# Expert up products of 128 + 64 contracted rows, and the first bias added by ScalarE behind the turning

## What is computed

```
xm = _ln(x, ln2_g, ln2_b).reshape(B * S, D)           # 32 * 82 rows of 192
probs = softmax(xm @ router_w.T + router_b)
topw, topi = top_k(probs, 2); topw = topw / sum(topw)
for e in range(8):
    h = gelu(xm @ w1[e] + b1[e], approximate=False)   # 192 -> 768
    y = h @ w2[e] + b2[e]                             # 768 -> 192
    out = out + combine[:, e:e + 1] * y
x = x + out
```

## Time and profile before

| | |
|---|---|
| runs | 1379.35 us median of 3 (1374.2 to 1379.79) |
| the profiled execution | 1381.3 us, its span 1379.5 us, mean granted clock of TensorE 0.941 |
| TensorE (PE) busy, share of the span | 1219.3 us, 88% |
| VectorE (DVE) | 1016.1 us, 74% |
| GpSimd (POOL) | 742.8 us, 54% |
| ScalarE (ACT) | 686.8 us, 50% |
| of the costliest groups, in the expert stage: L2258 up | 143.6 us |
| L2277 down | 109.3 us |
| L2267 flip | 40.0 us |
| L2309 affine | 38.3 us |
| L2315 Gelu | 38.9 us |
| L2347 copy to hT | 46.0 us |

### The profile page before, as it was taken

How to read it: one execution, slowest core, us unless ns; L and a number is a source line. 1 busy time by engine, 2 the same in 40 slices (tenths; PEclk the granted TensorE clock), 3 DMA queues, 4 the chain that set the end, 5 groups by cost and what they waited for, 6 DMA issues and landing times.

```text
span 1379.5 us, 19671 instructions
## 1 busy us (share of the span) xinstructions
PE 1219.3 (88%) x5828; PEld 787.5 (57%) x5829; DVE 1016.1 (74%) x2150; ACT 686.8 (50%) x1467; POOL 742.8 (54%) x469
## 2 busy tenths in 40 slices
PE   7976876659898989899987789999999899999996
PEld 4432343225454545545443568888888677777774
DVE  5998797989899999999999646778788553333332
ACT  1355433576777777686855246545452332222221
POOL 3147642886869696969788300145455474222222
PEclk9997878798999999999999999999998699999998
DMA  6200012340413223140410001122122132222221
GB/s 183 59 1 0 31 34 97 96 147 15 133 50 98 70 77 111 36 146 0 146 33 1 1 31 42 43 67 59 56 69 71 33 68 46 37 38 36 36 36 21
DMA packets 72801, 81.19 MB, mean 59 GB/s; under 512 B 13282, under 2 KB 64705, under 8 KB 72721
## 3 DMA queue, kind: packets, MB, share of 16 engines
q1 hardware_dynamic: 53386, 69.29, 15.9%
q0 software_dynamic: 17152, 9.24, 4.9%
q10 hardware_dynamic: 2184, 1.72, 0.5%
HBM read 48.87 MB, written 30.01 MB: 57 GB/s over the span
## 4 chain that ended last, share of the span: by engine, by line
PE 60%; DVE 20%; ACT 10%; issue 6%; POOL 2%; DMA 1%; DVEq 0%; SPq 0%; ACTq 0%; POOLq 0%
PE ps L2258 10%; PE ps L1040 7%; PE ps L2277 7%; DVE hs L1324 6%; PE ps L1642 3%; PE ps L1700 3%; PE ps L951 3%; PE ps L1715 3%; PE ps L275 2%; PE ps L2267 2%; ACT ps L1193 2%; PE ps L268 2%; PE ps L1017 2%; DVE ps L205 2%; PE ps L976 2%
## 5 line engine op out<-in xcount | busy, mean ns | idle before, releaser
L1442 POOL TENSOR_TENSOR Bx<-dtz,Bb 128x984 f32<-128x984 f32 x128 | 288.2, 2270 | 45.8 <-DVE hs L1324 31.8
L1324 DVE TENSOR_TENSOR_SCAN hs<-ps,Bx 128x492 f32<-128x492 f32 x256 | 287.6, 1164 | 21.9 <-POOL Bx L1442 12.6
L1193 ACT ACTIVATE ps<-dt,A 128x324 f32<-128x324 f32 (+1 forms) x512 | 211.5, 456 | 79.2 <-DVE hs L1324 77.0
L1040 PE MATMUL ps<-hs,b_id 128*128 128x492 f32 x512 | 238.6, 589 | 12.0 <-DVE y L1291 9.3
L2377 POOL DMA_INDIRECT out<-yt,dest x48 | 74.7, 1556 | 168.8 <-DVE yt L2363 156.4
L1334 DVE TENSOR_TENSOR hs<-hs,ps 128x984 f32<-128x984 f32 x128 | 150.2, 1174 | 2.5 <-issue 0.6
L2258 PE MATMUL ps<-W,xT 97*128 (+1 forms) x384 | 143.6, 518 | 2.9 <-issue 1.6
L1040 PEld LDWEIGHTS ps<-hs,b_id 128*128 128x128 f32 x512 | 93.0, 195 | 79.6 <-issue 74.2
L2347 DVE COPY hT__6147<-ps 128x768 f32<-128x768 f32 x48 | 46.0, 958 | 111.3 <-PE ps L2267 108.8
L2277 PE MATMUL ps<-W,hT__6147 128*128 x576 | 109.3, 327 | 0.8 <-DVE yb L2357 0.8
L2315 ACT ACTIVATE hb<-ps 128x768 f32<-128x768 f32 x48 | 38.9, 810 | 142.5 <-PE ps L2258 142.5
(11 more groups left out here) (277 smaller groups left out, 2404.1 us busy)
## 6 DMA issues: line engine op xcount, KB each, us to landing
Bb<-b_rows SPq DMA_DIRECT2D x32, 656.0 KB, 6.7
buckets<-b_zero SPq DMA_DIRECT2D x8, 2288.0 KB, 15.2
xg<-buckets SPq DMA_DIRECT2D x48, 104.0 KB, 1.9
xc<-in_xcol SPq DMA_DIRECT2D x4, 1176.0 KB, 9.3
W<-in_w1d SPq DMA_DIRECT2D x8, 582.0 KB
W<-in_w2d SPq DMA_DIRECT2D x8, 576.0 KB
out<-H SPq DMA_DIRECT2D x8, 246.0 KB
H<-P SPq DMA_DIRECT2D x8, 147.0 KB
```

The source lines that it names most:

```text
L1040: mm = pe.matmul(ps[:, BANK_Y + h, 0:HALF], ident[:], f2(hs[:, s % LONG])[:, h * HALF:(h + 1) * HALF], start=s == 0, stop=s == STATE - 1)
L1193: a = act.activation(ps[:, BANK_A + h, c:c + w].rearrange("p (g t) -> p g t", t=S)[:, :, 1:S], dt[:, (par + t // STATE) % 2, m, g0 * S:g1 ...
L1324: v.tensor_tensor_scan(f2(hs[:, t % LONG])[:, c], ps[:, BANK_A + h, 0:HALF], f2(Bx[:, t % RING])[:, c], 0.0, ALU.mult, ALU.add).then_inc(s ...
L1442: g.tensor_tensor(Bx[:, t % RING], dtz[:, p], Bb[:, p, t % STATE, :].rearrange("p (a n) -> p a n", a=1).broadcast_to([128, NI, N]), ALU.mu ...
```

## The change

- The turned tile lies as 128 x 128 (columns 0 to 127 of the row) and, from columns 64 to 191, once more 128 x 128, of which the upper 64 partitions are columns 128 to 191. ScalarE writes `xT` in three activations: all 128 rows; the 64 upper rows to partitions 64 to 127; the same 64 rows to partitions 0 to 63.
- W1 is laid out as 128 rows of all 768 columns, and behind them 384 more columns that hold the last 64 rows: of columns 0 to 383 in partitions 0 to 63, of columns 384 to 767 in partitions 64 to 127. For the second half VectorE copies the 64 x 384 of the tile's expert to `wh` (`high_rows`).
- The up is two products of 128 rows, one for each half h, and then two of 64 rows, at partitions 0 to 63 for h = 0 and 64 to 127 for h = 1. TensorE waits for `wh` as well.
- The bias leaves W1. VectorE copies the result of the up to `hb` unchanged (ScalarE does so for tiles 0 and 1, `lift`). After the flips ScalarE writes `hT` with six Gelus of 128 x 128, each with its column of `b1` as the bias; b1 now lies along the partitions. VectorE's copy to `hT` is gone.
- ScalarE's step j is now hidden(j), affine(j+2); before, it was hidden(j+1), affine(j+2). ScalarE reads the tile's expert from `te`. In the interleaved part hidden(0) moves behind affine(2).
- VectorE's step j: the copy to `hb` of tile j+1, high_rows(j+2), keep_tail(j+2), then the output of down(j-1) as before.
- One more DMA loads `b1` (128 x 48 numbers), behind that of b2. The memory has places for `wh` and `e_b1`.

```diff
                 for k in range(2):
-                    mm = pe.transpose(ps[0:HD, turned(j), k * 128:(k + 1) * 128], xg[:, p, k * HD:(k + 1) * HD], ident[:])
+                    mm = pe.transpose(ps[:, turned(j), k * 128:(k + 1) * 128], xg[:, p, k * 64:k * 64 + 128], ident[:])
                 mm.then_inc(s_tx, 1)
 
             def up(j, p, e):
 
                 pe.wait_ge(s_xT, j + 1)
-                if isinstance(j, int) and j == 0:
-                    pe.wait_ge(s_cst, 1)
+                pe.wait_ge(s_wh, j + 1)
                 at_least(pe, s_ge, j)
                 for h in range(2):
-                    for k in range(2):
-                        c_ = slice(0, HD + k)
-                        mm = pe.matmul(ps[:, UP + h, 0:384], xT[c_, p, k, :],
-                                       W1[c_, k, bass.ds(e, 1), h * 384:(h + 1) * 384].rearrange("p a n -> p (a n)"),
-                                       start=k == 0, stop=k == 1)
+                    pe.matmul(ps[:, UP + h, 0:384], xT[:, p, 0, :],
+                              W1[:, bass.ds(e, 1), h * 384:(h + 1) * 384].rearrange("p a n -> p (a n)"), start=True, stop=False)
+                for h in range(2):
+                    half = slice(64 * h, 64 * h + 64)
+                    w = wh[half, p, :] if h else W1[half, bass.ds(e, 1), DFF:W1_ROW].rearrange("p a n -> p (a n)")
+                    mm = pe.matmul(ps[:, UP + h, 0:384], xT[half, p, 1, :], w, start=False, stop=True)
                 mm.then_inc(s_h, 1)
...
             def affine(j, p):
                 act.wait_ge(s_tx, j + 1)
-                for k in range(2):
-                    a = act.activation(xT[0:HD, p, k, :], ps[0:HD, turned(j), k * 128:(k + 1) * 128], ACT.Identity,
-                                       bias=vec[0:HD, V_LN2_B + k:V_LN2_B + k + 1], scale=vec[0:HD, V_LN2_G + k:V_LN2_G + k + 1])
+                high = slice(64, 128)
+                act.activation(xT[:, p, 0, :], ps[:, turned(j), 0:128], ACT.Identity, bias=vec[:, V_E_B:V_E_B + 1], scale=vec[:, V_E_G:V_E_G + 1])
+                for rows in (high, slice(0, 64)):
+                    a = act.activation(xT[rows, p, 1, :], ps[high, turned(j), 128:256], ACT.Identity,
+                                       bias=vec[high, V_E_B + 1:V_E_B + 2], scale=vec[high, V_E_G + 1:V_E_G + 2])
                 a.then_inc(s_xT, 1)
 
+            def expert(j):
+                return act.value_load(te[0:1, bass.ds(j, 1)] if not isinstance(j, int) else te[0:1, j:j + 1],
+                                      min_val=0, max_val=EXPERTS - 1)
+
+            def lift(j, p):
+                act.wait_ge(s_h, j + 1)
+                act.activation(hb[:, p, :].rearrange("p (a n) -> p a n", a=2), ps[:, UP:UP + 2, 0:384], ACT.Copy).then_inc(s_ge, 1)
+
             def hidden(j, p):
-                act.wait_ge(s_h, j + 1)
-                act.activation(hb[:, p, :].rearrange("p (a n) -> p a n", a=2), ps[:, UP:UP + 2, 0:384], ACT.Gelu).then_inc(s_ge, 1)
+                if isinstance(j, int) and j == 0:
+                    act.wait_ge(s_b1, 16)
+                    act.wait_ge(s_tab, 1)
+                if isinstance(j, int) and j == FIRST:
+                    act.wait_ge(s_tab, 2)
+                e = expert(j)
+                act.wait_ge(s_ht, j + 1)
+                for k in range(KF):
+                    a = act.activation(hT[:, p, k, :], ps[:, FLIPPED + k // 3, (k % 3) * 128:(k % 3 + 1) * 128], ACT.Gelu,
+                                       bias=b1[:, k, bass.ds(e, 1)])
+                a.then_inc(s_hT, 1)
 
             def step(j, p4):
                 p = p4 % 2
-                if is_tile(j + 1):
-                    hidden(j + 1, 1 - p)
+                if is_tile(j):
+                    hidden(j, p)
                 if is_tile(j + 2):
                     affine(j + 2, p)
...
+            def high_rows(j, p):
+                e = expert(j)
+                v.tensor_copy(wh[64:128, p, :], W1[64:128, bass.ds(e, 1), DFF:W1_ROW].rearrange("p a n -> p (a n)")).then_inc(s_wh, 1)
+
...
-                if is_tile(j):
-                    v.wait_ge(s_ht, j + 1)
-                    v.tensor_copy(hT[:, p].rearrange("p (a k) n -> p a (k n)", a=2), ps[:, FLIPPED:FLIPPED + 2, 0:384]).then_inc(s_hT, 1)
+                if isinstance(j, int) and j == 0:
+                    v.wait_ge(s_h, 1)
+                elif is_tile(j + 1):
+                    v.wait_ge(s_h, j + 2)
+                    v.tensor_copy(hb[:, 1 - p, :].rearrange("p (a n) -> p a n", a=2), ps[:, UP:UP + 2, 0:384]).then_inc(s_ge, 1)
+                if is_tile(j + 2):
+                    high_rows(j + 2, p)
...
+    w1 = t["ffn_w1"].transpose(1, 0, 2)
+    a["w1d"] = np.concatenate([w1[0:128], np.concatenate([w1[128:192, :, 0:384], w1[128:192, :, 384:768]])], axis=2)
+    a["b1d"] = t["ffn_b1"].reshape(8, 6, 128).transpose(2, 1, 0)
```

More of the change, by code:

```diff
@@ L81 @@
 V_HF_NORM = 123
-V_N = 125
+V_E_G = 125
+V_E_B = 127
+V_N = 129
 CH = 4
@@ L644 @@
 KF = DFF // 128
+W1_ROW = DFF + DFF // 2
 U32 = mybir.dt.uint32
@@ L1489, with attention @@
 assert (FULL_ROUNDS * G * S * 2 - EXPERTS * 127) // 128 >= FIRST
-def attention(nc, ctx, block, at, ps, fr, left, H, out, xs, W1, W2, te, to, ident, vec, w1d, w2d, b2d):
+def attention(nc, ctx, block, at, ps, fr, left, H, out, xs, W1, W2, te, to, ident, vec, w1d, w2d, b1d, b2d):
     if True:
@@ L1583, in _ @@
             for e in range(EXPERTS):
-                sp.dma_start(W1[:, :, e, :], w1d[:, :, e, :]).then_inc(s_e, 16)
+                sp.dma_start(W1[:, e, :], w1d[:, e, :]).then_inc(s_e, 16)
                 sp.dma_start(W2[:, :, e, :], w2d[:, :, e, :]).then_inc(s_e, 16)
@@ L1595, in _ @@
             sp.dma_start(ex.b2[:], b2d.rearrange("(a e) d -> a e d", a=1).broadcast_to([128, EXPERTS, D])).then_inc(s_b2, 16)
+            sp.dma_start(ex.b1[:], b1d).then_inc(ex.s_b1, 16)
             t = ex.loads(sp)
@@ L1820, in _ @@
             step(i, par, 0)
-            t.hidden(0, 0)
+            t.lift(0, 0)
             route(i, par, 0)
@@ L1824, in _ @@
             step(i, par, 2)
-            t.hidden(1, 1)
+            t.lift(1, 1)
             t.affine(2, 0)
+            t.hidden(0, 0)
             gate_exp(ROUNDS - 2)
@@ L2074, in _ @@
             t = ex.vector(v)
-            t.ones()
             step(i, par, 0)
+            v.wait_ge(s_e, 32 * EXPERTS)
+            t.high_rows(0, 0)
+            t.high_rows(1, 1)
             t.keep_tail(0, 0)
@@ L2317, in step @@
             def step(j, p4):
                 p = p4 % 2
-                if is_tile(j + 1):
-                    hidden(j + 1, 1 - p)
+                if is_tile(j):
+                    hidden(j, p)
                 if is_tile(j + 2):
                     affine(j + 2, p)
-            t.affine, t.hidden, t.step = affine, hidden, step
+            t.affine, t.lift, t.hidden, t.step = affine, lift, hidden, step
             t.rest = lambda: rest_of(act, step, FIRST)
@@ L2329, in vector @@
             t = Stage()
-            def ones():
-                v.memset(xT[HD:HD + 1], 1.0).then_inc(s_cst, 1)
             def expert(j):
@@ L2363, in step @@
                     v.tensor_scalar(yt[:, n, :], yb[:, 1 - p, :], tail[:, n, bass.ds(e_out, 1)], None, ALU.mult).then_inc(s_yt, 1)
-            t.ones, t.keep_tail, t.step = ones, keep_tail, step
+            t.high_rows, t.keep_tail, t.step = high_rows, keep_tail, step
             t.rest = lambda: rest_of(v, step, FIRST)
@@ L2461, in _layout @@
     cols += [thirds(t["attn_b_dt"]), thirds(t["attn_D_skip"]), thirds(_heads(bq)), thirds(_heads(bk)), np.arange(128, dtype=f32)[:, None]]
-    cols += [_two_thirds(t["attn_w_norm1"]), _two_thirds(t["attn_w_ffn_norm"])]
+    cols += [_two_thirds(t[n]) for n in ("attn_w_norm1", "attn_w_ffn_norm", "ffn_ln2_g", "ffn_ln2_b")]
     a["vecs"] = np.concatenate(cols, axis=1)
@@ L2547, in places @@
     heads2, top = stack(top, ("E", 2 * HEADS * S * F), ("PT", 2 * HEADS * S * F))
-    w_experts, end = stack(top, ("W1", 2 * EXPERTS * DFF * F), ("W2", KF * EXPERTS * D * F))
-    tiles, top = stack(heads["kB"], ("xg", 2 * RW * F), ("xT", 4 * 128 * F), ("yb", 2 * D * F), ("yt", 4 * D * F), ("b2", EXPERTS * D * F),
+    w_experts, end = stack(top, ("W1", EXPERTS * W1_ROW * F), ("wh", DFF * F), ("W2", KF * EXPERTS * D * F))
+    tiles, top = stack(heads["kB"], ("xg", 2 * RW * F), ("xT", 4 * 128 * F), ("e_b1", KF * EXPERTS * F), ("yb", 2 * D * F), ("yt", 4 * D * F), ("b2", EXPERTS * D * F),
                        ("tail", 4 * (EXPERTS + 1) * F), ("dest", 4 * F))
@@ L2579, in program @@
             tok_ctx.close()
-            W1 = nc.alloc_sbuf_tensor_at("W1", [HD + 1, 2, EXPERTS, DFF], F32, offset=at["W1"])
+            W1 = nc.alloc_sbuf_tensor_at("W1", [128, EXPERTS, W1_ROW], F32, offset=at["W1"])
             W2 = nc.alloc_sbuf_tensor_at("W2", [128, KF, EXPERTS, D], F32, offset=at["W2"])
@@ L2583, in program @@
             to = nc.alloc_sbuf_tensor_at("to", [1, TILES + 1], I32, offset=at["to"])
```

(2 more changed lines are left out.)

10 lines of the change are left out of this document (3 added, 7 removed).

## The result

The changed kernel takes 1424.99 us (median of 4 runs, 1422.17 to 1427.1) against 1379.57 us for the kernel before in the same comparison: a ratio of 1.0333, 95% interval 1.0304 to 1.0362. It is slower by 45 us, where 29 us were forecast: inside the stated range, but above 1398 to 1420, which the prediction gave as the range of the ring alone. The profiled execution took 1425.23 us with a span of 1423.3 us. The same kernel measured a second time took 1419.59 us, 40 us more than the kernel before beside it.

What follows compares the result with a forecast made beforehand. The prediction took a ring of waits over TensorE and ScalarE in the expert loop as the bound. The profiled 1381.3 us plus 26 (loop) plus 3 (before tile 6) gave 1410.3, forecast as a 1408 us median, range 1390 to 1436.

Steps and rivals of the forecast that it cites:

- the ring: Expert loop: TensorE and ScalarE wait on each other in turn; period 6.32 us against 5.68, 26 us over 41 periods; chance 0.61.
- The up: Expert loop, TensorE: two products of 128 rows and two side-by-side of 64 take 2.33 us, 0.36 us less than before.
- The six Gelus: Expert loop, ScalarE behind the flips: six activations with a bias column, 0.25 us from start to start, 1.50 us in all.
- the affine: Expert loop, ScalarE ahead of the up: three activations without overlap take 1.38 us; the pair took 0.80 us.
- The step that failed: VectorE's order of lift, weights, tail, then down(j-1) output was said to meet each wait before TensorE stands still.
- the early stretch: Before tile 6: three or four longer periods and little more, 3 us, bounds 0 and 8.
- something in the early stretch slips by more than 8 us: Before tile 6: one of the conditions under which the prediction called its forecast wrong.
- slow Gelus: Rival: a bias address from a register stops overlap, each Gelu 0.35 us or more; 25 us more, 1433 us; chance 0.14.
- serial halves: Rival: the up's two 64-row halves run one after the other; 27 us more, 1435 us; chance 0.03.
- overlapping affine: Rival: affine takes 1.15 us for 1.38, no give-back at the flips, nothing early; 1392 us; chance 0.12.
- The clock stayed at 1.00: Answers the rival that TensorE's clock falls as it idles a sixth of each tile; 45 us more, 1453 us; chance 0.04.
- TensorE stays the bound: Rival: flip to up takes at most 2.44 us, TensorE's own 5.25 us sets the period; 18 us less, 1361; chance 0.06.

Runs made afterwards that it cites:

- the two other traces of the same early code: The changed kernel measured once more, unaltered, 1419.59 us; and the changed kernel with each Gelu's bias read at a fixed address, 1418.82 us.
- the other order: Changed kernel with turn(j+2) ahead of up(j+1) on TensorE and affine(j+2) ahead of hidden(j) on ScalarE: 1375.75 us, ratio 0.9935.

## Why the prediction was right, and where it was not

**The ring, term by term.** The up was put at 2.33 us and took 2.33 (1240.02 to 1242.35). The part from the start of the up to the landing of the flips was 3.25 and is 3.21. I had given 0.10 us back at the flips behind the halves; it is 0.06. The six Gelus were 1.50 us until the affine starts, and are 1.52; the affine was 1.38 and is 1.42; the delay from its end to the up was 0.15 and is 0.14. The term that was off most is the start of the first Gelu behind the flips, put at 0.04 us from VectorE's copy and measured as 0.13, since its address comes from a register. The sum was 6.32 us and the period is 6.42. In 41 periods that makes 30 us where I had 26.

**Which row to take.** For the affine I had chosen the row with the same form (a change of the start partition, no overlap) against full overlap, and the form decided: L2316 gives way 0.50 us after its start, not 0.35. For the Gelus I had taken the row of this kernel, 0.25 us, and the trace has 1.52 us for six, 0.25 each. The Trainium skill, "ScalarE: Activation LUTs", What ACT_TABLE_LOAD costs, gives 0.294 us for one as an estimate from its figures; here the measurement and the page differ, and the measurement stands. The up takes 2.33 us where six record times of 0.324 are 1.94: 0.39 us more, of which 0.10 is the late second record behind a wait. By the Trainium skill, "TensorEngine Tiling (Array Packing)", Key Properties, a change of the mode drains the array. The other 0.29 us fit that, but a drain as such is in no row.

**The step that failed** is the sentence that VectorE's order "has each wait met before TensorE stands still". It is true of the loop, where the copy of 64 x 384 ends long before its up and takes 0.36 us, not up to 0.96. I had looked at the loop alone. In the early stretch the same copy is queued behind `step(i, par, 0)` and behind `rank`, whose own waits are for TensorE, so that TensorE waits for a 0.36 us copy that VectorE starts only at 1081.29. My rule was to name what is queued behind a waiting instruction; the new wait of TensorE (`s_wh`) should have been followed back through VectorE's queue at each place where it is issued, above all for the first three tiles in the hand-ordered part. I had put this stretch at 3 us, bounds 0 and 8; it is 12.0 us in the profiled execution and 16.0 and 6.4 us in the two other traces of the same early code. With two copies moved ahead it is 5.6 us (67.4 against 61.8), and what the copies cost by themselves is sure only at the first up, 7.7 to 10.5 us. The clock of this stretch the prediction had left out altogether.

**The sum.** Forecast 26 + 3, measured 30.2 + 12.0 + 1.7 of unchanged code - 0.2 = 43.8 us of span. The direction and the mechanism of the loop were right, with the loop's loss put 14% too small, and the early stretch is four times what was forecast in this trace, twice to five times over the three. By the prediction's own words, "something in the early stretch slips by more than 8 us", that part of it was wrong (it slipped by more in two of the three traces). That the total still lies inside 1390 to 1436 is in part luck: the room above 1420 was there for slow Gelus and serial halves, which did not come, and the early stretch filled it.

**The rivals.** Slower Gelus, overlapping affine and serial halves are out by the rows above. The clock stayed at 1.00 in the loop with TensorE busy for 41.65 of 50 us; ahead of the loop it was 0.79 from the reduction to tile 6's up, and 0.78 there in the kernel before. That TensorE stays the bound needed 2.44 us or less from flip to up; it is 3.21 (1243.23 to 1246.44). But the rival's period, 5.25 us with TensorE alone, was near to what the other order reaches: 5.11.

## What to carry to other kernels

A busy engine's share, even 49.97 of 50 us, doesn't say that its work is the bound: add up the ring of waits around it, landing to landing, and cost each part of an edit on that ring, with small activations by their distance from start to start. Work that is moved to an idle engine is free only if the order lets it lie beside something; here the change cost 0.74 us a tile with nine activations in the ring, and with the turn first the same nine cost nothing: the period of 5.11 us is the 5.42 us of the kernel before in that order, less 0.36 us of shorter products, plus 0.05 us at the flips. Two traces of one early stretch can differ by more than the loss that one looks for, so its causes have to be read at single waits. A new wait has to be followed through the other engine's queue at every place where it is issued, the hand-ordered start first of all.

## What the runs showed of the hardware

An activation whose bias is addressed by a register started 0.13 us behind the landing of the flips it waited for, with a fixed address 0.03 us; the five behind it ran at 0.25 us either way. Activations of 128 columns from PSUM that stay on the same partitions and have one column operand (a bias) follow each other by 0.25 us; where the start partition changes they don't overlap (0.47 us between the two activations of L2318 that last 0.45; no run changes the partition alone). And in the up that started behind a wait the second fp32 record was 0.10 us late (eight records in 2.85 us against 2.75 us without the wait), which I had not counted as part of the hole.
